# Query phase and attention in one block: key jobs ahead of the queries, position bias from a 24 KB table

## The reference, cut to what matters

```python
q = shape(layernorm(x) @ wq, T)      # B=8, H=16 heads of 32, T=128
k = shape(ctx @ wk, S)               # S=2048
v = shape(ctx @ wv, S)
bias = rel_bias[bucket(s - t)]       # a function of s - t alone
scores = einsum('bhtd,bhsd->bhts', q, k) + bias
attn = einsum('bhts,bhsd->bhtd', softmax(scores), v)
x = x + attn.transpose(...) @ wo
```

## Time and profile before

| | |
|---|---|
| median of 3 runs | 2054.47 us (2053.71 to 2055.05) |
| profiled execution, its own time | 2055.39 us |
| its span, first to last instruction | 2053.6 us |
| PE, PEld busy | 1886.2 us (92%), 1431.3 us (70%) |
| DVE, ACT, POOL busy | 1130.7, 777.9, 804.0 us |
| all transfers | 210.82 MB |

### The profile page before, as it was taken

The page is one execution under the profiler, slowest core; times in us unless marked ns, Lnnn a source line. Parts: engine busy times, 40 slices in busy tenths (PEclk is TensorE's granted clock), DMA queues, the critical chain, the costliest instruction groups (busy, mean ns, idle before and its releaser), DMA issues. The chain is left out here.

```text
span 2053.6 us, 40698 instructions
## 1 busy us (share of the span) xinstructions
PE 1886.2 (92%) x17102; PEld 1431.3 (70%) x17102; DVE 1130.7 (55%) x2160; ACT 777.9 (38%) x1295; POOL 804.0 (39%) x641
## 2 busy tenths in 40 slices
PE   7599999999999999999999999579879998599995
PEld 3477777677677677677677777367657877499995
DVE  4244656656656556657556557464765233455553
ACT  1233434344344434344344334241244130355552
POOL 0114677668668677667667662000000000100001
PEclk9899999999999999999999999789989997699998
DMA  8622121121121122122122101210041004799993
GB/s 166 209 88 87 53 73 56 54 79 58 48 78 58 52 73 63 47 76 70 38 78 68 35 30 33 90 52 14 1 139 31 1 1 173 281 368 358 359 359 110
DMA packets 101126, 210.82 MB, mean 103 GB/s; under 512 B 9088, under 2 KB 33968, under 8 KB 95840
## 3 DMA queue, kind: packets, MB, share of 16 engines
q1 hardware_dynamic: 99488, 204.02, 29.4%
q0 software_dynamic: 1472, 4.40, 0.7%
HBM read 187.68 MB, written 20.71 MB: 101 GB/s over the span
## 5 line engine op out<-in xcount | busy, mean ns | idle before, releaser
L369 POOL TENSOR_TENSOR total<-total,probT 128x512 f32<-128x512 f32 x392 | 502.7, 1282 | 231.6 <-ACT probT L411 207.5
L488 DVE TENSOR_REDUCE negm<-bank 128x1 f32<-128x512 f32 x512 | 326.8, 685 | 179.4 <-PE bank L572 175.0
L469 DVE TENSOR_TENSOR probT<-bank,shift 128x512 f32<-128x512 f32 (+1 forms) x512 | 291.2, 615 | 216.2 <-PE bank L584 216.2
L411 ACT ACTIVATE probT<-probT 128x1024 f32<-128x1024 f32 x256 | 271.2, 1060 | 227.4 <-DVE probT L469 214.6
L405 ACT ACTIVATE v<-bank 128x512 f32<-128x512 f32 x128 | 76.4, 597 | 478.3 <-PE bank L552 478.3
L345 POOL TENSOR_TENSOR ctx_lo<-ctx_raw,ctx_hi 128x512 fp32r<-128x512 f32 x128 | 165.7, 1295 | 153.2 <-ACT ctx_hi L391 148.9
L552 PE MATMUL bank<-ctx_hi,wkv_hi 128*128 128x512 f32 x512 | 152.1, 419 | 22.5 <-ACT ctx_hi L391 22.5
L602 PEld LDWEIGHTS bank<-probT,v 128*32 128x32 f32 x4096 | 104.0, 109 | 94.0 <-ACT probT L411 92.0
L584 PEld LDWEIGHTS bank<-q,k 32*128 32x128 f32 x4096 | 126.0, 186 | 46.5 <-issue 44.1
L1348 POOL MEMSET zero_sb<- 128x512 f32 x1 | 0.5, 525 | 393.2 <-POOLq L1118 393.2
L552 PE MATMUL bank<-wkv_hi,ctx_hi 128*128 128x512 f32 x512 | 152.6, 420 | 0.0
(11 more groups left out here) (236 smaller groups left out, 2800.8 us busy)
## 6 DMA issues: line engine op xcount, KB each, us to landing
w_sb<-w SPq DMA_DIRECT2D x10, 4096.0 KB, 14.2
w_sb<-w SPq DMA_DIRECT2D x40, 1024.0 KB, 6.3
ctx_raw<-ctxT SPq DMA_DIRECT2D x128, 256.0 KB, 3.2
bias<-bias_scratch SPq DMA_DIRECT2D x32, 512.0 KB, 5.3
shift<-turned_bias SPq DMA_DIRECT2D x32, 512.0 KB, 5.1
slots<-zero_sb SPq DMA_DIRECT2D x17, 256.0 KB, 3.0
bias_scratch<-btab SPq DMA_DIRECT2D x1, 3072.0 KB, 34.2
down_w<-down SPq DMA_DIRECT2D x11, 256.0 KB, 2.6
```

Source lines behind the costliest of these rows:

```text
L369: pool.tensor_tensor(total[:, g], total[:, g], part, ALU.add).then_inc(add_step, 1)
L411: act.activation(pT[:, u % 2, j:j + 2], pT[:, u % 2, j:j + 2], ACT.Exp).then_inc(exp_done, 1)
L469: dve.tensor_tensor(pT[:, u % 2, j, i0:], sc[:, i0:], shift[:, g, j].unsqueeze(1).broadcast_to([P, ST - i0, T]), ALU.add).then_inc(shifted, 1)
L488: dve.tensor_reduce(negm[:, c, h:h + 1], sc[:], AX.X, ALU.max, negate=True).then_inc(max_done, 1)
```

## The change

The two phases become one block. The queue of loads starts with Wk and the first chunk of context, so that the key and value jobs of steps 0 to 3 come first. Statistics of x run beside them; x is turned in step 3; each of steps 4 to 11 projects the queries of one sequence, as 16 matmuls of 128 columns. Scores start in step 5, and in steps 6 to 9 a second set per step catches up. Buffers that attention does not use yet hold the start's data (`w_raw` in `v`, x in `probT`, Wq in `shift0`, turned x in `total` and `shift`). Queries of the first three sequences stay on the chip, five are stored.

The first 256 context rows of each sequence are given in reversed order. The bias is then a function of t + s: row t of the bias is 256 entries of the table from t + 1 on, and the turned bias is the same array. So the table is stored once (24 KB), and bias and turned bias are both read from it as 128 overlapping rows for each of 4 heads. The transposes of the bias, their copies, stores and the 2 MB read go away.

```diff
+STD_STEP = 2
+Q_STEP = STD_STEP + 2
+FIRST_SCORES = Q_STEP + 1
+SCORES_EARLY = {FIRST_SCORES + i: (2 * i - 1,) for i in range(1, FIRST_SCORES)}
+def main_scores(t):
+
+    return min(t - 1, 2 * (t - FIRST_SCORES))
...
-                sp.dma_start(env["bias_dram"][:], btab[:].unsqueeze(1).broadcast_to([H, T, BL])).then_inc(stored, 16)
...
+                def table_rows(g):
+                    return bass.AP(env["table_dram"].tensor, 1 + g * HG * BL, [[1, P], [BL, HG], [1, BW]])
...
-                    sp.dma_start(bias[:, i % 2], bass.AP(env["bias_dram"].tensor, T - 1 + (i % G) * HG * T * BL,
-                                                         [[BL - 1, T], [T * BL, HG], [1, BW]])
-                                 ).then_inc(bias_in[i % 2], 16)
+                    sp.dma_start(bias[:, i % 2], table_rows(i % G)).then_inc(bias_in[i % 2], 16)
...
-                    sp.dma_start(shift0[:, i % 2], env["turned_dram"][g]).then_inc(shift0_in[i % 2], 16)
+                    sp.dma_start(shift0[:, i % 2].rearrange("p j s t -> p j (s t)"), table_rows(i % G)
+                                 ).then_inc(shift0_in[i % 2], 16)
...
-                    if b == 0 and a in TURNED_KEPT:
-                        i = TURNED_KEPT.index(a)
-                        sp.wait_ge(turned_out, 2 * (i + 1))
-                        sp.dma_start(env["turned_dram"][i], shift0[:, i % 2]).then_inc(turned_kept[i % 2], 16)
-                    if a in (2, 3) and b < B:
-                        load_bias(b * G + a)
+                    if 3 <= t - Q_STEP < B:
+                        keep_q(t - Q_STEP)
+                    if a in ((5, 6) if b == 0 else (2, 3)) and b < B:
+                        load_bias(b * G + (a - 3 if b == 0 else a))
...
+                def keep_query(b):
+                    act.wait_ge(q_mm, b + 1)
+                    act.activation(q_home[b], misc[:].rearrange("p (g t) -> p g t", g=G), ACT.Copy).then_inc(q_done, 1)
...
-                    if 1 <= t <= LAST_T:
-                        maxima(t - 1)
+                    for a in SCORES_EARLY.get(t, ()):
+                        maxima(a)
+                    if FIRST_SCORES <= t <= LAST_T:
+                        maxima(main_scores(t))
...
+                def query(b):
...
+                    for g in range(G):
+                        for c in range(DC):
+                            mm = pe.matmul(misc[:, g * T:(g + 1) * T], wq[:, c, g * P:(g + 1) * P], xT[b // 4][:, b % 4, c, :],
+                                           start=(c == 0), stop=(c == DC - 1))
+                    mm.then_inc(q_mm, 1)
...
-                    if t in TURN_AT:
-                        turn_bias(TURN_AT.index(t))
-                    if 1 <= t <= LAST_T:
-                        scores(t - 1)
+                    if t == STD_STEP + 1:
+                        turn_x()
+                    if 0 <= t - Q_STEP < B:
+                        query(t - Q_STEP)
+                    if FIRST_SCORES <= t <= LAST_T:
+                        scores(main_scores(t))
```

More of the change, by code:

```diff
@@ L55, in ring_plan @@
                     at = count % RING_BANKS
-                    place[kind, first + j] = at
-                    user[kind, first + j] = last.get(at, ("none", 0))
-                    last[at] = (kind, first + j)
+                    place[kind, HG * n + j] = at
+                    user[kind, HG * n + j] = last.get(at, ("none", 0))
+                    last[at] = (kind, HG * n + j)
                     count += 1
@@ L215, in attention_phase @@
-def attention_phase(nc, env):
-    bank = env["bank"]
-    ring, misc, kv_bank, o_bank = bank[0:RING_BANKS], bank[5], bank[6], bank[7]
-    ident, wkv_hi, wkv_lo = env["ident"], env["wkv_hi"], env["wkv_lo"]
-    with ExitStack() as ctx:
-        def sb(name, shape, dt=F32):
-            return ctx.enter_context(nc.sbuf_tensor(name, shape, dt))
-        def sem(name):
-            return ctx.enter_context(nc.semaphore(name))
+        wkv_hi = sb("wkv_hi", [P, 2 * DC, D], F32R)
+        wkv_lo = sb("wkv_lo", [P, 2 * DC, D], F32R)
@@ L261, in attention_phase @@
         wo_mm, x_in, x_done, x_stored = sem("wo_mm"), sem("x_row_in"), sem("x_row_done"), sem("x_stored")
-        full = pT[:].rearrange("p u j i t -> p (u j i t)").rearrange("p (h w) -> p h w", h=H)
+        w_raw = v[:, 1:3].rearrange("p c s d -> p (c s) d")
+        ctx0 = k[:, 1]
+        xs = pT[:].rearrange("p u j i t -> p (u j i t)").rearrange("p (b d) -> p b d", b=B)
+        xT = [half[:].rearrange("p g j t -> p (g j t)").rearrange("p (b c t) -> p b c t", b=B // 2, c=DC)
+              for half in (total, shift)]
+        wq = shift0[:].rearrange("p u j s t -> p (u j s t)").rearrange("p (c n) -> p c n", c=DC)
+        onehot = x_row[0:NB, 0:BL]
+        table = aT[:].rearrange("p g t -> p (g t)")[0:H, 0:BL]
+        x_flat = x_row[:].rearrange("p (g t) -> p g t", g=G)
+        q_home = [q[:, b] for b in range(3)] + [k[:, 3, b - 3, :].rearrange("p (g t) -> p g t", g=G)
+                                                for b in range(3, 7)] + [x_flat]
         with nc.Block() as block:
@@ L669, in _ @@
                         scores_turned(t - LAG)
+                    for a in SCORES_EARLY.get(t, ()):
+                        scores(a)
                     if t < LAST_T:
@@ L685, in _ @@
                         project(t, 1)
+                    if t == 0:
+                        pe.wait_ge(table_in, 32)
+                        pe.matmul(misc[0:H, 0:BL], relb[:], onehot, start=True, stop=True).then_inc(table_mm, 1)
                     i = t - WO_STEP
```

201 lines of the change are left out of this document (128 added, 73 removed).

## The result

| | before | after |
|---|---|---|
| median | 2054.52 us (4 runs, 2053.71 to 2055.05) | 2024.56 us (4 runs, 2024.19 to 2025.79) |
| span of the profiled execution | 2053.6 us | 2022.4 us |
| start of the finish line (first transposed scores) | 187.31 us | 156.22 us |
| span behind the finish line | 1866.3 us | 1866.2 us |
| all transfers | 210.82 MB | 201.96 MB |

The ratio is 0.9857, with a 95% interval of 0.9842 to 0.9873: 30 us less, against a predicted 2023.5 us. All of it is won ahead of the finish line (31.1 us there); what follows has the length that it had.

What follows compares the result with a forecast made beforehand. TensorE was taken as the bound. Step 4 at 41.7 us plus 67.9, 16.05, 1.06, 28.8 and 0.5 put first transposed scores at 156.0 against 187.3; 31.3 us saved gave a median of 2023.5, range 2019 to 2035.

Steps and rivals of the forecast that it cites:

- The bound: From 200 to 1200 us TensorE is busy for all 1000 us; only its own work counts there.
- The loads' line: Start's load queue: 367 GB/s, 1.05 MB per 2.86 us, putting the fifth context piece at 18.7 us.
- The starved start: Rival: start's loads run at 265 GB/s, fifth piece 5.7 us later, 6 to 12 us lost, 2030 to 2036; 12%.
- What sets step 1: TensorE finishes its first jobs between 19.5 and 22; ScalarE allows no start before 19.9; 20.5 us taken.
- Steps 1 to 4: From 20.5 us: five jobs 14.2, turning x 4.2, job (3, values) 2.83; step 4 starts at 41.7.
- one of the prediction's signs of being wrong: After step 1: the forecast would be wrong if key copies on ScalarE waited for a context piece.
- Queries: Steps 4 to 11: 16 narrow matmuls take 3.6 us per query, 28.8 for eight; the cut costs nothing.
- The rival of narrow matmuls that do not overlap: Query matmuls: 0.277 us per record alone, 8.9 for a query, 42 more in all, 2066 us; 4%.
- Steps 4 to the finish line: From 41.7 to 156.0 us: jobs 67.9, scores 16.05, spreads 1.06, queries 28.8, bank waits 0.5.
- the ring's waits: Steps 6 to 9: scores opening a step can find the last bank not yet free, 0.5 us in all.
- The table: Bias loads of 512 KB from 6 KB land in 5.3 us, with 11.28 us from issue to use.
- The hot table's price: Rival: bias loads exceed 11.28 us, 14 loads each pass on the excess; at 16 us, 66 lost, 2090; 6%.

Runs made afterwards that it cites:

- the earlier step 1: Changed kernel with Wk and first context chunk in interleaved halves, first low parts on VectorE, key copy ahead of the fifth piece's rounding: 2023.29 us, ratio 0.9856.
- late bias loads: Changed kernel with the third and fourth bias load of sequences 2 to 8 issued a step late: 2027.46 us, 2.9 more than the changed kernel.

## Why the prediction was right

It gave 2023.5 us; the median is 2024.56, 1.1 above, with the finish line at 156.22 for a predicted 156.0. (Its own sum gives 2055.4 - 31.3 - 0.9 = 2023.2; it doesn't say where the other 0.3 comes from.) That the finish line fits to 0.2 is in part luck: step 4 began 0.8 us earlier than predicted, and the stretch from there took 1.0 longer. Its steps in order:

- **The bound** is TensorE, before and after: shown by the queries done twice, of whose 28.6 us (8 x 3.58) 28.3 came out. With x moved ahead a late start was passed on whole, which agrees, though x's chain was late there too.
- **The loads' line** (367 GB/s) put the fifth piece at 18.7; it was there at 18.37. The first key job was predicted at 11.6 and came at 11.29. The starved start did not come in the changed kernel.
- **What sets step 1**: 20.5 predicted, 20.04 measured. The prediction had two terms, TensorE's own jobs (done between 19.5 and 22) and a lower bound by ScalarE (19.9, the fifth piece and two passes), and left open which comes last. It was TensorE's jobs: the key copy was done at 19.49, TensorE at 20.04. Within these jobs the third part of the first waited for GpSimd's low parts, as the prediction saw (15.25 for its 14.9). With these low parts on VectorE and the copy ahead of the piece (the earlier step 1) the start came forward to 19.20.
- **Steps 1 to 4**: predicted 20.5 to 41.7, 21.2 us; measured 20.04 to 40.93, 20.9. The turning of x took 4.30 for the 4.2 predicted. The prediction saw the normalising end near 35 and "under job (3, keys) but for its end"; the wait was 0.37. The normalising was mis-sized, 4.73 us for the 3.74 taken from the kernel before, and the five jobs ahead of it took 13.7 for 14.2, so that no room was left: x's chain ended just behind TensorE's jobs. ScalarE waited for the seventh and eighth context pieces (0.55 and 0.24 us), one of the prediction's signs of being wrong, but TensorE did not wait for the key copies behind them.
- **Queries**: 3.6 predicted from the expert's narrow matmuls; the pitch is 3.48 without scores behind and 3.67 with them. The rival of narrow matmuls that do not overlap is out.
- **Steps 4 to the finish line**: predicted 156.0 - 41.7 = 114.3, measured 115.3. Two terms were small by 0.4 each: the ring's waits came to 2 x 0.46 = 0.9 for 0.5, and the queries to 3.48 + 7 x 3.67 = 29.2 for 28.8. Steps 6 to 9, for which it gave about 11.4, took 12.1 twice, with a ring wait each, and 11.6 twice.
- **The table** lands in 5.0 us (3.5 to 7.7) where 5.3 was taken, and in 5.5 in the run with the table alone: 128 rows that start 4 bytes apart take as long, within 0.3 us, as rows spread over 3 MB. The Trainium skill (DMA: Bandwidth & Descriptors, "Latency and other measured facts") has half rate, 103 in place of 207 GB/s, at row pitches of 4 and 8 MiB, which it puts down, as an inference, to streams of partitions that meet on the same memory channels. Such a slowing does not show for these rows, 4 bytes apart: 5.0 us, not the 10.6 that the prediction estimated for it.
- **The hot table's price** was wrong. The prediction charged each of 14 loads with what it is late. Of 14 loads issued some 9 us late, 7 made VectorE wait, 28.2 us in all, and one made TensorE wait. Passed on whole, as the prediction has it, that were 28 us; it was 2.9 by the medians. At up to 4 us of lateness that rival costs far less than it gave. With 1.1 us of room left in the third sequence it would cost more soon after, and that was not run.
- **The split of the gain**, which the prediction did not give, is 7.5 for the table put in alone and some 22 for the merging on top of it.

## What to carry to other kernels

Where one engine is the limit in the steady part, look for its idle time at the two ends, and fill it with work of the next stage that needs only the first loads; the gain can be added up in its own matmuls, and it is passed on to the end as long as that engine's queue stays full. A late transfer is not priced by its lateness times its count: see in each place what the bound engine has queued that does not need it. And when a start is brought forward, look for the next chain that arrives just in time (here x's statistics, square root and normalising), since it can take the gain back within a few steps.

## What the runs showed of the hardware that was not expected

- **The clock column at the start.** In the window from 11.29 to 20.04 the granted clock stands as 1.00, yet its first eight matmuls took 1.91 to 2.07 us for four, and later ones 1.07: by the durations TensorE was at the lower of its levels, 1.2 GHz, after 11.29 us without a matmul. In the late bias loads the same durations stood beside a granted 0.70. The Trainium skill (TensorE: Matmul & The Clock Gate, "Part 1: The HAM clock gate (the "warmup" mystery)") tells that the slow level is the default and activity releases it; the durations agree, the column at the start does not.
- **A short wait costs more than itself.** 2.71 us without matmuls cost some 4.3 (late bias loads), since the next matmuls were slow. After 1.48 us without (the earlier step 1) the 12 transposes took 1.82 and the four matmuls behind them 1.17, as in the changed kernel.
- **Small pieces were cheap to move and could be dear to issue.** 512 KB in pieces of 128 bytes landed in 7.3 us and of 64 bytes in 7.9, for 5.0 in rows of 1 KB; but where two loads of 64-byte pieces were issued one behind the other at the start they took SyncE 4.84 us, for 0.93 in the changed kernel, and the 256 KB piece behind them 5.98, for 0.50. Most issues stayed short (median 0.43 for a bias load in both kernels), and a long one isn't the small pieces' alone: in the changed kernel the 64 KB identity matrix, behind x's two loads, took 2.48 to issue. The Trainium skill (DMA: Bandwidth & Descriptors, "Specifications") wants 512 bytes or more for the full rate; the landing times of 7.3 and 7.9 us for 5.0 agree.
